# Cross-attention and mixture-of-experts layer: value bias carried by the attention's tail, another order of the prologue and its loads, and GpSimd making the low weight parts of experts 5 to 16

## The reference

```python
q = layernorm(x) @ Wq + bq;  k = ctx @ Wk + bk;  v = ctx @ Wv + bv
attn = softmax(where(mask, q @ k.T / sqrt(256), -inf))
x = x + attn @ v
xf = layernorm(x)
scores = sigmoid(l2norm(xf) @ l2norm(gate_w).T)          # 16 experts, the top 8 kept and normalised
routed = sum over e of combine[:, e] * (silu(xf @ w_gate[e]) * (xf @ w_up[e])) @ w_down[e]
x = x + routed + silu(xf @ sw_gate) * (xf @ sw_up) @ sw_down
```

## Time and profile before

| | |
|---|---|
| median of 3 runs | 651.84 us (650.86 to 651.99) |
| the profiled execution | 650.85 us |
| its span | 648.7 us |
| PE busy | 634.6 us, 98% |
| DVE, ACT, POOL busy | 472.7, 235.7, 294.7 us |
| PE's clock by slices of 16 us | full in nearly all |

### The profile page before, as it was taken

How to read it: one execution, slowest core, us unless ns; L and a number is a source line. 1 busy time by engine, 2 the same in 40 slices (tenths; PEclk the granted TensorE clock), 3 DMA queues, 4 the chain that set the end, 5 groups by cost and what they waited for, 6 DMA issues and landing times.

```text
span 648.7 us, 10466 instructions
## 1 busy us (share of the span) xinstructions
PE 634.6 (98%) x3688; PEld 551.5 (85%) x3688; DVE 472.7 (73%) x941; ACT 235.7 (36%) x500; POOL 294.7 (45%) x275
## 2 busy tenths in 40 slices
PE   8898999999999999999999999999999999999997
PEld 7576888889888888888888898888888888888886
DVE  3779897868967588766868689675887768575443
ACT  5644444333243323433243332433234332432221
POOL 2517687333743356333563337433464334423333
PEclk9999899999999999999999999999999999999999
DMA  7265663424225324053244342263240531242100
GB/s 212 68 168 193 175 176 79 149 70 151 63 35 198 90 83 97 24 174 107 74 89 131 89 148 64 36 198 98 73 98 22 177 107 42 56 132 98 65 1 33
DMA packets 112655, 67.19 MB, mean 104 GB/s; under 512 B 80996, under 2 KB 102396, under 8 KB 112604
## 3 DMA queue, kind: packets, MB, share of 16 engines
q1 hardware_dynamic: 111516, 65.74, 36.0%
q10 hardware_dynamic: 1088, 0.79, 0.4%
HBM read 55.79 MB, written 10.42 MB: 102 GB/s over the span
## 4 chain that ended last, share of the span: by engine, by line
PE 91%; DVE 5%; issue 2%; ACT 1%; POOL 1%; POOLq 0%; ACTq 0%; DVEq 0%
PE y_ps L393 9%; PE gate_ps L395 9%; PE gate_ps L394 9%; PE up_ps L395 9%; PE up_ps L394 9%; PE gate_ps L393 9%; PE up_ps L393 9%; PE y_ps L394 9%; PE y_ps L395 9%; PE f_ps L538 2%; DVE hs L1155 1%; DVE W L999 1%; PE up_ps L402 1%; PE f_ps L575 1%; PE f_ps L393 1%
## 5 line engine op out<-in xcount | busy, mean ns | idle before, releaser
L1351 POOL TENSOR_TENSOR hidden<-hidden,cb 128x512 f32<-128x512 f32 x128 | 193.9, 1515 | 278.5 <-DVE hidden L1149 234.3
L866 ACT ACTIVATE hidden<-gate_ps 128x512 f32<-128x512 f32 x136 | 81.3, 598 | 292.9 <-PE gate_ps L395 292.9
L1145 DVE SCALAR_TENSOR_TENSOR hidden<-hidden,gate_ps 128x512 f32<-128x512 f32 x136 | 92.7, 681 | 102.9 <-ACT hidden L866 102.7
L393 PE MATMUL y_ps<-W,hs 128*128 128x256 f32 x544 | 154.7, 284 | 5.0 <-DVE hs L1155 5.0
L394 PE MATMUL y_ps<-W,hs 128*128 128x256 f32 x544 | 151.6, 279 | 0.0
L395 PE MATMUL y_ps<-W,hs 128*128 128x256 f32 x544 | 151.4, 278 | 0.0
L1155 DVE TENSOR_TENSOR hs<-hidden,hs 128x512 fp32r<-128x512 f32 x136 | 111.1, 817 | 21.8 <-ACT hs L873 21.6
L393 PEld LDWEIGHTS y_ps<-W,hs 128*128 128x128 f32 x544 | 102.2, 188 | 13.6 <-ACT hs L873 5.0
L393 PE MATMUL gate_ps<-xT,W 128*128 128x512 f32 x272 | 107.9, 397 | 0.0
L395 PE MATMUL gate_ps<-xT,W 128*128 128x512 f32 x272 | 107.6, 396 | 0.0
L394 PE MATMUL gate_ps<-xT,W 128*128 128x512 f32 x272 | 107.3, 395 | 0.0
(11 more groups left out here) (162 smaller groups left out, 664.0 us busy)
## 6 DMA issues: line engine op xcount, KB each, us to landing
cb<-c_rows SPq DMA_DIRECT2D x64, 512.0 KB, 4.8
blocks<-in_x_dram SPq DMA_DIRECT2D x28, 128.0 KB, 2.9
xin<-in_x_dram SPq DMA_DIRECT2D x7, 512.0 KB, 4.1
t_rows<-blocks SPq DMA_DIRECT2D x28, 128.0 KB, 2.7
xs<-t_rows SPq DMA_DIRECT2D x7, 512.0 KB, 3.5
out_dram<-x SPq DMA_DIRECT2D x7, 512.0 KB, 6.2
p_rows<-blocks SPq DMA_DIRECT2D x28, 80.0 KB, 2.3
stage<-in_L_ffn_w_gate_dram SPq DMA_DIRECT2D x16, 128.0 KB, 2.5
```

The source lines that it names most:

```text
L393: mm(ps, lh, rh, start=first and i == 0, stop=False)
L866: af(ew[:, i, :], gate_ps[:, i, :], ACT.Tanh, scale=0.5).then_inc(tanh_done, 1)
L1145: V_.scalar_tensor_tensor(out=ew[:, i, :], in0=ew[:, i, :], scalar=1.0, in1=gate_ps[:, i, :], op0=ALU.add, op1=ALU.mult).then_inc(silu_don ...
L1351: pg.tensor_tensor(h[:, i, :], ew[:, i, :], cb[:, pair % PLACES, (e - 1) % 2, :], ALU.mult) \
```

## The change

It does several things at once.

1. The value bias. Column 154 of the probabilities, the first padding column, now holds each row's sum of exponentials (`esum` is that column; `exps` accumulates into it). The value tails get bv as their row 26 through one more matmul with one row (`bv_places` x `bv_row`), so attention's tail multiplies the sum by bv, and the later division by the sum leaves bv. `add_bv` on POOL goes, with its wait in `residual`; bv is loaded as one row of 1 KB in place of a 128 KB broadcast.
2. The negated maximum is written by the reduction itself; L1070 goes.
3. The order of the prologue on all engines: both halves' exps before the value copies, `load_stage(3)`, `load_stage(4)` and `load_x_blocks(1)` before `move_v_tails`, `turn_router` behind `values(1)`, `split_hi(3)` and `split_hi(4)` earlier, `split_lo(3)` earlier, `ln2(0,1)` ahead of `ln2_scale(0,0)`.
4. POOL makes the low parts of experts 5 to 16. In the laps, `split_hi(s+5)` on ACT stands behind `hidden_hi(s+1)`.
5. `add_bias` goes from lap 9.5 to 12.5. In the last chunk gate(16) and up(16) stand ahead of down(13).

```diff
-POOL_SOON = dict(add_bias=(9.5,), ln1_std=(11.5, 11.5), add_bv=(13.5, 14.5))
-POOL_FIRST = dict(ln1_std=(.5, .5), add_bv=(2.5, 4.5))
+POOL_SOON = dict(add_bias=(12.5,), ln1_std=(11.5, 11.5))
+POOL_FIRST = dict(ln1_std=(.5, .5))
+        esum = att[:, :, KEYS]
-        POOL_SPLITS = (0, 1, 6, 8, 10, 12, 14, 16)
+        POOL_SPLITS = (0, 1, 5, 6, 7, 8, 9, 10, 11, 12, 13, 14, 15, 16)
...
+            sp.dma_start(bv_row[:], bv.partition_broadcast(1)).then_inc(bv_loaded, 16)
-            sp.dma_start(bvb[:], bv.partition_broadcast(P)).then_inc(bv_loaded, 16)
             for e in range(STAGES):
                 load_stage(e)
+            load_stage(STAGES)
+            load_stage(STAGES + 1)
+            load_x_blocks(1)
             move_v_tails()
-            for e in range(STAGES, STAGES + 3):
-                load_stage(e)
-            load_x_blocks(1)
             load_x(1)
+            load_stage(STAGES + 2)
...
+                mm(y_ps[:, 0, D:2 * D], bv_places[:], bv_row[:], start=False, stop=True).then_inc(vt_made, 1)
...
             attend(0, 0)
-            turn_router()
             attend(0, 1)
             values(1, y_ps[:, 0, 0:D])
+            turn_router()
...
+                    if not ahead and s + AHEAD == NE - 1:
+                        gate(c, NE - 1)
+                        up(c, NE - 1)
                     down(c, s)
...
             exps(0, 0)
-            write_vt_hi()
+            exps(0, 1)
+            vt_hi_first()
             write_v_hi(0, y_ps[:, 0, 0:D])
-            exps(0, 1)
             probs_hi_first(0)
             probs_hi_first(1)
+            write_vt_hi()
...
                         front(s, c + 1)                # ACT
+                    if s + 1 < NE or ahead:
+                        hidden_hi(c, s + 1)
                     if c == 0 and s + EARLY < NE:
                         split_hi(s + EARLY)
-                    if s + 1 < NE or ahead:
-                        hidden_hi(c, s + 1)
...
-                V_.tensor_reduce(rsum[:, 2 * q:2 * q + 2], att[:, 2 * q:2 * q + 2, 0:KEYS], AX_X, ALU.max)
-                dve.wait_ge(maxes, upto(c, 2, q + 1))
-                V_.tensor_scalar(nmax[:, 2 * q:2 * q + 2], rsum[:, 2 * q:2 * q + 2], -1.0, None, ALU.mult)
+                V_.tensor_reduce(nmax[:, 2 * q:2 * q + 2], att[:, 2 * q:2 * q + 2, 0:KEYS], AX_X, ALU.max, negate=True)
...
-            router_scaled()
-            write_vt_lo()
+            vt_lo_first()
             write_v_lo(0, y_ps[:, 0, 0:D])
             sum_reciprocal(0)
             probs_lo_first(0)
             probs_lo_first(1)
+            write_vt_lo()
+            router_scaled()
...
+                    if s + 1 < NE or ahead:
+                        hidden_lo(c, s + 1)            # DVE, now ahead of its split_lo
                     if c == 0 and s + EARLY < NE and s + EARLY not in POOL_SPLITS:
                         split_lo(s + EARLY)
...
-            add_bv(0, 0)                               # POOL
-            add_bv(0, 1)
```

More of the change, by code:

```diff
@@ L59, in xattn_moe_kernel @@
     QUADS = P // SQ
-    assert S == 2 * TOK and KD == 2 and H == P and 0 < TAIL <= PAD and E % 4 == 0 and NE % 2 == 1 and B == 4
+    assert S == 2 * TOK and KD == 2 and H == P and 0 < TAIL < PAD and E % 4 == 0 and NE % 2 == 1 and B == 4
     assert REST <= 512 and 2 * E * TILES == P and B * PAD == P
@@ L80, in xattn_moe_kernel @@
         small = sb("small", [P, 12, TILES])
-        var_eps, rstd, nmax, esum, rsum, rsq, nsq, inorm, ssum, srec = (small[:, i, :] for i in range(10))
+        var_eps, rstd, nmax, rsum, rsq, nsq, inorm, ssum, srec = (small[:, i, :] for i in range(9))
         top8 = sb("top8", [P, TILES, 8])
@@ L92, in xattn_moe_kernel @@
         V = sb("V", [P, B, 2, D], F32R)
-        bvb = sb("bvb", [P, D])
+        bv_row = sb("bv_row", [1, D])
+        bv_places = sb("bv_places", [1, B * PAD])
         keep = sb("keep", [P, S // P, KEYS])
@@ L177, in xattn_moe_kernel @@
          c_read, bn_step, pool_step, std_step, norm_step) = (
-            sem(n) for n in ("ln1_stats", "ln1_rstd", "x_swapped", "p_swapped", "x2_swapped", "t1_turned", "t1_read", "bias_added", "x_biased", "scored",
-                             "scaled", "maxes", "maxed", "exped", "rsummed", "p_turned", "p_hi", "p_lo", "attended",
+            sem(n) for n in ("ln1_stats", "ln1_rstd", "x_swapped", "p_swapped", "x2_swapped", "t1_turned", "t1_read", "bias_added", "scored",
+                             "scaled", "maxed", "exped", "rsummed", "p_turned", "p_hi", "p_lo", "attended",
                              "x2_made", "ln2_stats", "ln2_rstd", "inv_norms", "ln2_done", "t2_turned", "t2_hi",
@@ L483, in value_tails @@
                 for k in range(KD):
-                    ins = mm(y_ps[:, 0, D:2 * D], ctxTt[:, k, :], wv_in[:, k, :], start=k == 0, stop=k == KD - 1)
-                ins.then_inc(vt_made, 1)
+                    mm(y_ps[:, 0, D:2 * D], ctxTt[:, k, :], wv_in[:, k, :], start=k == 0, stop=False)
+                pe.wait_ge(bv_loaded, 16)
+                pe.wait_ge(pads_set, 2)
+                mm(y_ps[:, 0, D:2 * D], bv_places[:], bv_row[:], start=False, stop=True).then_inc(vt_made, 1)
             def values(b, to):
@@ L692, in _ @@
                         front(s, c + 1)
-                    if (s + AHEAD < NE or ahead) and not (c == 0 and s == 1):
+                    if (s + AHEAD < NE - 1 or ahead) and not (c == 0 and s == 1):
                         gate(c, s + AHEAD)
@@ L779, in write_vt_hi @@
                     ins = af(Vtail[row:row + PAD, 0, :], y_ps[0:PAD, 0, D:2 * D], ACT.Copy)
-                ins.then_inc(vt_split, 1)
+                ins.then_inc(vt0_split, 1)
+            def write_vt_hi():
+                act.wait_ge(v_lo, 1)
                 af(vt[:, HI, :], y_ps[:, 0, D:2 * D], ACT.Copy).then_inc(vt_split, 1)
@@ L917, in _ @@
             write_v_hi(1, y_ps[:, 0, 0:D])
+            split_hi(3)
             bias_row_rest()
             router_hi()
-            split_hi(3)
+            split_hi(4)
             t2_hi_first(0)
@@ L923, in _ @@
             read_a_rest(0)
-            split_hi(4)
             read_z(0)
@@ L971, in mean_wq, with vt_lo_first, write_vt_lo @@
                 V_.tensor_scalar(wq_sum[:, KD:2 * KD], wq_sum[:, 0:KD], -1.0 / D, None, ALU.mult).then_inc(wq_mean, 1)
[L973 to L974 removed]
+            def vt_lo_first():
+                dve.wait_ge(vt0_split, 1)
                 dve.wait_ge(v_hi, 1)
                 V_.tensor_tensor(Vtail[2 * PAD:STACK, 0, :], y_ps[0:PAD, 0, D:2 * D], Vtail[0:PAD, 0, :].bitcast(F32),
[L977 removed]
+                                 ALU.subtract).then_inc(vt0_split, 1)
+            def write_vt_lo():
+                dve.wait_ge(vt_split, 1)
                 V_.tensor_tensor(vt[:, LO, :], y_ps[:, 0, D:2 * D], vt[:, HI, :].bitcast(F32), ALU.subtract) \
@@ L1220, in _ @@
             residual(0, 1)
+            ln2(0, 1)
             ln2_scale(0, 0)
-            ln2(0, 1)
             ln2_scale(0, 1)
@@ L1228, in _ @@
             split_lo(2)
+            split_lo(3)
             sum_logits(0)
@@ L1234, in _ @@
             hidden_lo(0, 0)
-            split_lo(3)
             write_v_lo(2, f_ps[:, 0, 0:D])
@@ L1268, in setup @@
                 pg.memset(ctx_tail, 0.0).then_inc(tail_zeroed, 1)
-                pg.memset(ident[:], 0.0).then_inc(pool_step, 1)
+                pg.memset(ident[:], 0.0)
+                pg.memset(bv_places[:], 0.0).then_inc(pool_step, 1)
                 pg.memset(minus_half[:], -0.5)
@@ L1364, in first @@
                     ln1_std(1, part)
-                for part in due(POOL_FIRST, "add_bv", at):
-                    add_bv(1, part)
             def soon(at, c):
@@ L1373, in soon @@
                     ln1_std(c, part)
-                for part in due(POOL_SOON, "add_bv", at):
-                    add_bv(c, part)
             pool.sem_inc(h_done, FREE)
```

34 lines of the change are left out of this document (11 added, 23 removed).

## The result

The changed kernel takes 653.89 us (median, 652.73 to 655.9) beside 651.91 for the kernel before on the same chip: ratio 1.0034, 95% interval 1.0022 to 1.0046, so some 2.2 us slower. The executions of one kernel lie up to 7.5 us apart, and two of the experiments' executions, of 1058.7 and 1458.81 us, are left out of the ratios. The profiled executions have spans of 651.2 and 648.7 us: +2.5.

A forecast was written before the change was run, and what follows sets the result against it. PE, busy 98%, bounds the kernel, so only prologue, chunk 0 and tail matter. down(13) 2.6 us later, with the prologue's gain included, less 1.1 in the tail gives +1.5: 653.3 us, the case's own range 651.1 to 654.8.

The forecast's parts named there:

- a ring of in-order queues: Chunk 0: POOL's weighted, ACT's hidden_hi and split_hi, POOL's split_lo, next weighted; 4.59 us a lap against PE's 4.13.
- Logits at 31.4: Prologue: routing logits start at 31.4 us, 2.5 us sooner (1.5 to 3.5).
- A lap of 4.59 us: Chunk 0: one lap of weighted, hidden_hi, split_hi and split_lo with hand-overs takes 4.59 us, 0.46 over PE's.
- 12 laps, 8.1 us of roots and 1.7 of collisions: Chunk 0, laps 0 to 11: extra POOL work (two ln1_std, ln2_std, inverse_norm) adds 8.1 us; DVE-POOL collisions with both exceptions, 1.7.
- 3.1 us from weighted(13) to down(13): End of chunk 0: POOL and ACT steps, then either hidden_lo or read_z, whose turn precedes down(13); 3.1 us.
- down(13) at 113.1: End of chunk 0: down(13) starts at 113.1 us, 2.6 later than before (0.9 to 3.1).
- PE's waits before lap 7 cost nothing: Chunk 0: early PE waits are free since the ring overtakes PE; PE idles 2 us before down(9), 3 before down(10).
- Nothing in chunks 1 to 7: Chunks 1 to 7: removing add_bv and moving add_bias gain nothing, as they stand in POOL's free time.
- The tail, -1.1: Last chunk: earlier gate(16) and up(16) let down(16) start at 642.7 in place of 643.81, 1.1 us won.
- the second: Rival, prologue: attention starts sooner but logits do not, so the ring starts 2.5 us later; +4.0, 655.8 us; chance 0.08.
- The third, collisions in most laps: Rival, chunk 0: POOL and DVE collide, 0.3 to 0.4 us in each of twelve laps; +5, 657 us; chance 0.15.
- The first, that the ring isn't closed: Rival, chunk 0: PE stays the bound, its waits and slow clock go; -8.2, 643.6 us; chance 0.17.

The follow-up runs named there:

- its own experiment: Changed kernel with gate(16) and up(16) of the last chunk back behind down(13): 656.1 us, ratio 1.0048 to the kernel before.
- 643.75 version: Changed kernel with chunk 0's laps as before (old shares of low parts, splits ahead of hidden_hi and hidden_lo): 643.75 us, ratio 0.9876 to the kernel before.

## Why the prediction was right

The forecast was +1.5 us, the profiles show +2.5, and the mechanism was the one named: a ring of in-order queues that takes from chunk 0 more than the prologue and the tail give. Point by point:

- *Logits at 31.4.* They came at 31.78: 2.14 us won, not 2.5. The second scaling came at 28.87, 1.45 us sooner and not 1.9. The exps moved from 17.83 to 16.80 (1.0 for 1.2; what they had waited for was POOL's split, which held the sign change), and the one-row bias matmul costs more than the 0.4 taken: 0.69 for its two. The nine DMAs ended at 31.9, not 30. The same view as the earlier trace rows, all engines:

```profile
16.80 0.44 ACT L829 ACTIVATE att<-att,small 128x154 f32<-128x154 f32 x1
...
17.05 0.69 PE L492 MATMUL y_ps<-bv_row,bv_places 1*128 1x256 f32 x2
...
24.28 7.60 SPq L319 DMA_DIRECT2D Vtail<-vt  x9
...
28.87 0.74 DVE L1032 TENSOR_SCALAR xn<-x,meanvar,small 128x256 f32<-128x256 f32 x2 [0.60 <-POOL small L1311]
...
31.78 0.61 PE L582 MATMUL f_ps<-xT,G 128*32 128x512 f32 x2
```

- *weighted(1) at 45.15.* 45.63: the same half microsecond.
- *A lap of 4.59 us.* 4.56 to 4.59. (PE's own lap, 12 x 0.228 + 12 x 0.115, is 4.12 and not 4.13, which changes nothing.)
- *12 laps, 8.1 us of roots and 1.7 of collisions.* From 45.63 to 111.31 it is 65.68 us. Twelve laps of 4.58 are 55.0, so the extras are 10.7, not 9.8: lap 5 took 6.24 (70.69 to 76.93), 1.66 over a plain lap and above the 0.9 to 1.4 foreseen. ACT had waited 2.03 us for the probabilities' DMA ahead of their high parts, and POOL's split ran 2.40 in place of 1.85. In lap 8 the collision came, but DVE paid it: ln2_scale took 2.25 us for its two (0.73 in the kernel before), POOL's split 1.94, and POOL's lap is 2.02 over a plain one, the inverse norm alone. Lap 11 had one that I missed: DVE's t2_lo stretched POOL's first two small operations to 0.51 and 1.03 (their twins read 0.19 and 0.69), which put weighted(13) 0.7 later. The rows of lap 8, then DVE of lap 11:

```profile
90.82 2.25 DVE L1032 TENSOR_SCALAR xn<-x,meanvar,small 128x256 f32<-128x256 f32 x2
90.99 1.94 POOL L1303 TENSOR_TENSOR W<-stage,W 128x768 fp32r<-128x768 f32 x1 [1.47 <-ACT W L809]
...
107.20 2.52 DVE L1068 TENSOR_TENSOR xT<-xs,xT 128x512 fp32r<-128x512 f32 x2 [0.56 <-ACT xT L824]
```

- *3.1 us from weighted(13) to down(13).* 3.33, and it was the second branch, read_z and the turn: PE's wait of 0.59 names ACT's zT. The first was close: add_bias in its new place (POOL, 112.56 to 113.94) held hidden_lo, which took 1.20 us from 113.30 and ended at 114.50.
- *down(13) at 113.1.* 114.64: 0.5 from the start, 0.8 from the extras, 0.2 from the end. This is the term that was mis-sized, +4.2 for +2.6, and it lies outside the 0.9 to 3.1 that I gave it. (My own terms reach 0.9 + 1.4 + 0.5 = 2.8; for the last 0.3 the working has no source.)
- *PE's waits before lap 7 cost nothing.* So it was: waits of 1.48 and 1.34 us before down(2) and attend left no mark, since weighted(13) follows from POOL's laps alone. PE idled 1.81 us ahead of down(9) at 91.05 and 0.65 ahead of down(10), 2.5 in place of the 5 foreseen; at 0.83 of full clock between 90 and 100 us PE took part of that time as slow matmuls.
- *Nothing in chunks 1 to 7.* Not quite: a chunk takes 75.63 us between turns (190.34 to 568.48 in five) against 75.73 before, some 0.6 us in all. The 643.75 version shows it too (75.61), so it isn't from the laps; no run separated its cause.
- *The tail, -1.1.* The last chunk and tail gave 1.13, and its own experiment 1.3. hidden_hi(16) waited for PE's y_ps, as foreseen.
- Sum: 4.18 - 0.57 - 1.13 = +2.48, the difference of the spans. Chunk 0 was 1.6 us short, and the 0.57 that I had put at nothing took a third of that back: this part of the agreement is luck.

The rivals: the prologue did what it said (2.14 us), which leaves out the second. The third, collisions in most laps, fell for the changed kernel: the plain laps show none. The first, that the ring isn't closed, was wrong of this kernel. I had priced it at 643.6; the changed kernel with ACT's order undone, which opens the ring and leaves the shares, takes 647.35. That the version with the laps as before gives 643.75 is not this rival's case, and the agreement with 643.6 is chance. The laps' rearrangement costs 12.1 us of span in the kernel before (660.8 - 648.7) and 10.5 in the changed one (651.2 - 640.7). Of the 10.5, 7.2 go when ACT's order alone is undone (644.0) and 3.3 stay with the shares.

On collisions, the Trainium skill ("SBUF — State Buffer", Who interferes with whom) says that a DVE instruction with two SBUF inputs and a GpSimd instruction that reads SBUF exclude each other for their whole length. The runs agree, both ways: hidden_lo at 1.92 for 0.69 us, and weighted at 1.74 for 1.29, in the version with ACT's old order.

Open: which edits save the 2.4 us of waits and the slow clock in chunk 0, beyond the prologue's shift, in the 643.75 version. By one trace each, the sign change accounts for about 1 us of down(13)'s 6.4 and split_lo(3)'s place for about 0.8; that add_bv left POOL's laps 2 and 4, and that the loads come sooner, were not tried against each other.

## What to carry to other kernels

Before reordering queues that wait on each other, write down the loop: which instruction on each engine stands behind which, until the chain comes back to the first. Its sum is the lap, and if it is longer than PE's lap the kernel runs at the loop's pace, with every engine involved well under full. To break it, take out one edge (an order, or who does a part) and look at what the other queues, the loads above all, then wait for; and test each part of a bundle by itself, since here four parts gave 8 us and the fifth took 10 back. And when a tiny instruction takes far longer than its twins elsewhere, look at what POOL has in hand at that moment before blaming the instruction.

## What the hardware showed that was not expected

- The sign change of 128x2, 0.17 us in the later chunks, took 1.58 us when it started inside POOL's split, and ended 0.02 us behind it.
- A matmul over one row isn't cheaper than one over 128: the bias's two records of 256 columns took 0.69 us, four of the value matmul before them, of the same width, 1.02.
- The same nine DMAs took SP 5.69 us to issue before, 7.60 after and 6.70 in the version with the old order of loads.
- After a wait of 5.03 us PE had 0.54 of full clock in a stretch of 5 us, near the lower of its two levels (1.2 of 2.4 GHz); two logits matmuls took 1.62 us there in place of 0.62.
